# A flamingo block (WKV, FFN, cross attention, MoE) on one core: order of the maxima and the big fill on SP's queue, and the shared expert's first products

## The reference

```python
x = x + tanh(g_xattn[0]) * wkv(layernorm(x), ctx)
x = x + tanh(g_ffn[0]) * ffn(layernorm(x))                  # 704 hidden, silu gate
x = x + tanh(g_xattn[1]) * attention(layernorm(x), ctx)     # 16 heads of 8, source and target mask, softmax
x = x + tanh(g_ffn[1]) * moe(layernorm(x))
# attention: q, k, v are projections of 128 channels over 256 positions (a batch is read as 128 x 256)
dot = einsum('bhdt,bhds->bhts', q, k) / sqrt(8)
dot = mask * dot - (1 - mask) * 1e6
out = einsum('bhts,bhds->bhdt', softmax(dot) * mask, v)
# moe: 8 experts, top 1, 256 slots each, 352 hidden, and a shared expert that takes every token
shared = (silu(xt @ sw1) * (xt @ sw3)) @ sw2
```

## Time and profile before

| what | value |
|---|---|
| median of three runs | 559.36 us |
| the profiled execution | 558.33 us |
| its span | 556.5 us |
| mean granted clock of TensorE | 0.972 |
| the profile's block 2 (attention with the FFN's end) | about 153 to 407.6 us |
| from the experts' block to the end | 407.6 to 556.5 us |

### The profile page before, as it was taken

The page is one execution under the profiler, slowest core; times in us unless marked ns, Lnnn a source line. Parts: engine busy times, 40 slices in busy tenths (PEclk is TensorE's granted clock), DMA queues, the critical chain, the costliest instruction groups (busy, mean ns, idle before and its releaser), DMA issues. The chain is left out here.

```text
span 556.5 us, 10469 instructions
## 1 busy us (share of the span) xinstructions
PE 483.7 (87%) x3384; PEld 264.7 (48%) x3384; DVE 379.6 (68%) x768; ACT 247.5 (44%) x478; POOL 229.2 (41%) x303
## 2 busy tenths in 40 slices
PE   2859999998898788988898989787979989899994
PEld 2634564745533433333333433332434545688873
DVE  4986879788589777788788888795757433333331
ACT  2732233121232177878788888677711100133321
POOL 2753224142367165666555565412110730024424
PEclk9987999999999979999999999899999999999998
DMA  7747600000175525555556665510050241168753
GB/s 214 214 145 166 104 1 0 1 1 2 57 195 143 130 57 150 147 143 143 141 141 147 162 156 135 146 28 5 1 157 1 91 165 47 58 167 185 196 127 38
DMA packets 67254, 59.94 MB, mean 108 GB/s; under 512 B 10048, under 2 KB 62256, under 8 KB 67216
## 3 DMA queue, kind: packets, MB, share of 16 engines
q1 hardware_dynamic: 63424, 55.24, 36.9%
q0 software_dynamic: 3072, 4.21, 4.4%
q10 hardware_dynamic: 720, 0.00, 0.1%
HBM read 38.90 MB, written 22.50 MB: 110 GB/s over the span
## 5 line engine op out<-in xcount | busy, mean ns | idle before, releaser
L1175 DVE TENSOR_REDUCE MX<-psum 128x2 f32<-128x512 f32 x256 | 161.3, 683 | 34.4 <-PE psum L1054 33.4
L1215 ACT ACTIVATE HP<-psum 128x512 f32<-128x512 f32 x256 | 137.5, 598 | 56.4 <-PE psum L1068 55.4
L1054 PE MATMUL psum<-QKA 60*128 60x256 bf16 x512 | 83.7, 281 | 13.8 <-DVE MX L1175 10.1
L1068 PE MATMUL psum<-QKA 60*128 60x256 bf16 x512 | 79.4, 281 | 16.1 <-DMA QKA<-max_scr 12.6
L1141 PE MATMUL psum<-HP,VP 128*32 128x256 f32 x1024 | 84.0, 402 | 0.2 <-ACT HP L1215 0.2
L512 PE MATMUL psum<-space_a,space_w 128*128 128x512 f32 x160 | 75.0, 618 | 1.1 <-ACT space_a L497 0.8
L1054 PEld LDWEIGHTS psum<-QKA 60*128 60x128 bf16 x512 | 35.9, 96 | 69.3 <-DVE MX L1175 47.9
L1736 POOL DMA_INDIRECT out_x<-OE,to_u x16 | 25.0, 1564 | 75.7 <-ACT OE L1777 73.2
L512 PEld LDWEIGHTS psum<-space_a,space_w 128*128 128x128 f32 x160 | 30.3, 197 | 37.9 <-issue 35.3
L525 ACT ACTIVATE space_a<-psum,hgs 128x512 f32<-128x512 f32 (+1 forms) x24 | 15.6, 651 | 70.3 <-PE psum L512 47.8
L1875 PE MATMUL psum<-XT,WE 128*128 128x256 f32 (+1 forms) x192 | 44.3, 380 | 2.4 <-ACT XT L1761 1.6
(11 more groups left out here) (186 smaller groups left out, 735.3 us busy)
## 6 DMA issues: line engine op xcount, KB each, us to landing
QKA<-stack_scr SPq DMA_DIRECT2D x32, 480.0 KB, 5.4
stack_scr<-PARTS SPq DMA_DIRECT2D x32, 192.0 KB, 2.0
WE<-in_W SPq DMA_DIRECT2D x16, 352.0 KB
stack_scr<-PARTS SPq DMA_DIRECT2D x32, 128.0 KB, 1.9
XD<-dispatched SPq DMA_DIRECT2D x8, 258.0 KB, 3.7
X<-in_x SPq DMA_DIRECT2D x4, 512.0 KB, 5.6
CTX<-in_ctx SPq DMA_DIRECT2D x4, 512.0 KB, 8.2
MB<-in_mask SPq DMA_DIRECT2D x16, 128.0 KB, 5.7
```

Source lines behind the costliest of these rows:

```text
L1054: return pe.matmul(to[:, tt * T:(tt + 1) * T], QKA[rows, k, 0, h, tt * P:(tt + 1) * P], QKA[rows, k, 1, h, :], start=True, stop=True)
L1068: return pe.matmul(to[:, (m % 2) * T:(m % 2 + 1) * T], QKA[rows, k, 1, h, st * P:(st + 1) * P], QKA[rows, k, 0, h, :], start=True, stop=True)
L1175: dve.tensor_reduce(MX[:, par, head_of(n), :], src[:, :].rearrange("p (a s) -> p a s", a=2), axis=AX.X, op=ALU.max).then_inc(a_red, 1)
L1215: act.activation(PT[:, i % 2, st, 2 * half:2 * half + 2, :].rearrange("p j t -> p (j t)"), TBK3[THIRDS[m]], ACT.Exp).then_inc(a_exp, 1)
```

## The change

Seven edits.

1. SP, in each batch of the attention: the big fill is issued behind the maxima's store, the mask load and the maxima's way back, instead of ahead of them.
2. The turning of the maxima (mxT) goes from the end of slot 0 to slot 1, ahead of that slot's scores; it waits for the copy QK of batch b+4, since both use bank 7. The query projection goes from slot 6 to slot 7, and its copy QK on ScalarE from slot 7 to slot 0 of the next batch. NM goes from slot 0 to slot 1, behind that slot's exponentials.
3. Ahead of the first batch: the projection and QK of batch 4 and VectorE's Z3 for it are done before the slots; the projection of batch 3 is later.
4. The one wait of TensorE for both halves of the FFN's last x2 becomes a wait per score bank.
5. The layer norm statistics of the last group (dve_stats3) are cut in five steps and stand in slots of batches 0 to 2 (LAST_STATS); pool_power3 for it stands in batch 2.
6. Five of the shared expert's 24 products (group 0: piece 0 both sides, piece 1 both sides, piece 2's gate side) stand in the last slots of the attention (SHARED).
7. In block 3, HS has two buffers, and the products of group 1 are spread over the router's stretches. The loops over the groups on TensorE and VectorE are written out, ScalarE's covers groups 2 and 3.

```diff
--- before.py
+++ after.py
...
@@ -179,6 +181,16 @@
+        def gu_shared(pe, g, i, side, first=False):
+            m = width(i, EH)
+            if not first and side == 0:
+                pe.wait_ge(m_h, NH * (g - 1) + i + 1)
+            for h in range(2):
+                last = pe.matmul(bank[2 * i + side][0:m, :], (wsh1, wsh3)[side][:, h, i * P:i * P + m],
+                                 ZT4[:, h, bass.ds(GT * g, GT)], start=(h == 0), stop=(h == 1))
+            if side == 1:
+                last.then_inc(m_gu, 1)
+
...
@@ -661,13 +674,24 @@
+            def dve_one_of_last(dve, ch, i):
+
+                if i < GB:
+                    ch.do(dve.bn_stats(stats3[:, i, :], X[:, GB * G3 + i, :]))
+                    return
+                ch.wait()
+                alone(dve)
+                for t in range(GB):
+                    ch.do(dve.bn_aggr(mv3[:, GB * G3 + t, :], stats3[:, t, :]))
+                ch.wait()
+                dve.tensor_scalar(veps3[:, GB * G3:B], mv3[:, GB * G3:B, 1], EPS, None, ALU.add).then_inc(a_var, 1)
+
...
-            G3 = NG - 1
@@ -892,9 +916,9 @@
-                            pe.wait_ge(a_qk, 1)
-                            pe_proj_q(pe, 0, 2, QB[0])
...
+                            pe.wait_ge(s_x2, 1 + 2 * G3)
+                            pe_proj_q(pe, 0, 2)
@@ -1117,6 +1141,8 @@
+                        if first(GB * to_turn[0] + to_turn[1]) and p == 0:
+                            pe.wait_ge(s_x2, 1 + 2 * G3 + n + 1)
@@ -1160,7 +1186,7 @@
-                    pool.wait_ge(a_rstd, NG)
+                    pool.wait_ge(a_rstd, b // GB + 1 if isinstance(b, int) else NG)
@@ -1327,6 +1353,8 @@
+                SHARED = {(B - 1, 7): [(0, 0)], (B, 0): [(0, 1)], (B, 1): [(1, 0), (1, 1)], (B, 4): [(2, 0)]}
+                LAST_STATS = [2, 4, 10, 12, 18]
@@ -1346,8 +1374,6 @@
-                            if there(b, 3):
-                                sp_fill(sp, *at(g, k, 3))
@@ -1356,6 +1382,8 @@
+                            if there(b, 3):
+                                sp_fill(sp, *at(g, k, 3))
@@ -1375,7 +1403,7 @@
-                                act_qk(act, 2, QB[0])
+                                act_qk(act, 2)
@@ -1384,6 +1412,7 @@
+                        act_qk(act, AHEAD_Q)
@@ -1392,12 +1421,10 @@
-                            if p == 0 and there(b, 1):
+                            if p == 0 and not first(b) and there(b, AHEAD_Q):
+                                act_qk(act, b + AHEAD_Q)
+                            if p == 1 and there(b, 1):
...
-                            if p == 2 and first(b):
-                                act_qk(act, AHEAD_Q)
-                            if p == 7 and there(b, AHEAD_Z):
-                                act_qk(act, b + AHEAD_Z)
@@ -1426,18 +1453,17 @@
-                        pool_power3(pool, G3)
...
-                            if p == 0 and not first(b) and there(b, AHEAD_Q):
+                            if p == 0 and there(b, AHEAD_Q):
...
-                            if p == 2 and first(b):
-                                pool_masked(pool, *at(g, k, AHEAD_Q))
+                            if p == 3 and isinstance(b, int) and b == 2:
+                                pool_power3(pool, G3)
@@ -1457,25 +1483,26 @@
-                            if (b, p) == (0, 0):
-                                pe.wait_ge(a_qk, AHEAD_V)
...
+                            if (b, p) == (1, 4):
+                                pe.wait_ge(a_nm, 1)
+                                pe_proj_q(pe, 1, 0)
...
-                            if i == 1:
+                            if i == 3:
+                                pe.wait_ge(a_qk, AHEAD_V)
...
-                        pe.wait_ge(s_x2, 1 + 2 * NG)
@@ -1483,6 +1510,12 @@
+                            if p == 1 and there(b, 1):
+                                if there(b, AHEAD_Q):
+                                    pe.wait_ge(a_qk, b + AHEAD_Q + 1)
+                                else:
+                                    pe.wait_ge(a_x3, b - 1)
+                                pe_mxT(pe, *at(g, k, 1))
@@ -1492,21 +1525,6 @@
-                            if p == 0 and there(b, 1):
-                                if there(b, AHEAD_Q):
-                                    pe.wait_ge(a_qk, b + AHEAD_Q + (0 if first(b) else 1))
-                                else:
-                                    pe.wait_ge(a_x3, b - 1)
-                                pe_mxT(pe, *at(g, k, 1))
-                            if p == 1 and first(b):
-                                pe.wait_ge(a_nm, 2)
-                                pe_proj_q(pe, *at(g, k, AHEAD_Q))
-                            if p == 6 and there(b, AHEAD_Z):
-                                if first(b):
-                                    pe.wait_ge(a_qk, AHEAD_Z)
-                                else:
-                                    pe.wait_ge(a_x3, b)
-                                pe_proj_q(pe, *at(g, k, AHEAD_Z))
@@ -1515,6 +1533,17 @@
+                            if p == 7 and there(b, AHEAD_Z):
+                                if first(b):
+                                    pe.wait_ge(a_nm, 2)
+                                else:
+                                    pe.wait_ge(a_x3, b)
+                                pe_proj_q(pe, *at(g, k, AHEAD_Z))
+                            if isinstance(b, int) and (b, p) in SHARED:
+                                if (b, p) == (B - 1, 7):
+                                    pe.wait_ge(m_zt, 2 * G3)
+                                for piece, side in SHARED[(b, p)]:
+                                    gu_shared(pe, 0, piece, side, first=True)
@@ -1543,19 +1572,19 @@
+                        dve_z3(dve, AHEAD_Q)
...
-                        dve_stats3(dve, ln3, G3)
...
-                            if p == 1 and first(b):
-                                dve_z3(dve, AHEAD_Q)
...
+                            if isinstance(b, int) and 8 * b + p in LAST_STATS:
+                                dve_one_of_last(dve, ln3, LAST_STATS.index(8 * b + p))
@@ -1616,7 +1645,7 @@
-            HS = sbp("HS", [P, NH, GT])
+            HS = sbp("HS", [P, 2, NH, GT])
...
@@ -1745,14 +1772,16 @@
-                    tanh_shared(0, 0, first=True)
-                    tanh_shared(0, 1, first=True)
+                    for i in range(NH):
+                        tanh_shared(0, i, first=True)
+                    tanh_shared(1, 0)
...
-                    tanh_shared(0, 2, first=True)
-                    with act.Fori(1, NG) as g:
+                    tanh_shared(1, 1)
+                    tanh_shared(1, 2)
+                    with act.Fori(2, NG) as g:
...
@@ -1812,43 +1831,44 @@
-                                    last = pe.matmul(bank[6 + k][:, b * C:(b + 1) * C], HS[0:m, i, t * P:(t + 1) * P],
+                                    last = pe.matmul(bank[6 + k][:, b * C:(b + 1) * C], HS[0:m, g % 2, i, t * P:(t + 1) * P],
...
+                    gu_shared(pe, 0, 2, 1, first=True)
...
-                        gu_shared(0, 0, side, first=True)
+                        gu_shared(pe, 1, 0, side)
...
-                    for side in range(2):
-                        gu_shared(0, 1, side, first=True)
-
...
-                    gu_shared(0, 2, 0, first=True)
+                    gu_shared(pe, 1, 1, 0)
...
-                    gu_shared(0, 2, 1, first=True)
+                    gu_shared(pe, 1, 1, 1)
+                    gu_shared(pe, 1, 2, 0)
...
-                    with pe.Fori(0, NG - 1) as g:
+                    gu_shared(pe, 1, 2, 1)
+                    pe.wait_ge(m_pos, 1)
+                    down_shared(0)
+                    for g in range(1, NG - 1):
...
-                            gu_shared(g + 1, 0, side)
-                        pe.wait_ge(m_pos, 1)
+                            gu_shared(pe, g + 1, 0, side)
...
-                                gu_shared(g + 1, i, side)
+                                gu_shared(pe, g + 1, i, side)
@@ -1919,15 +1939,16 @@
-                        dve.scalar_tensor_tensor(out=HS[0:m, i, :], in0=H1[0:m, i, :], scalar=0.5,
+                        dve.scalar_tensor_tensor(out=HS[0:m, g % 2, i, :], in0=H1[0:m, i, :], scalar=0.5,
...
+                    hidden_shared(ch, 0, 0)
...
-                    hidden_shared(ch, 0, 0)
...
+                    hidden_shared(ch, 0, 2)
@@ -1965,7 +1986,7 @@
-                    hidden_shared(ch, 0, 2)
+                    hidden_shared(ch, 1, 0)
@@ -2014,14 +2035,15 @@
-                    before = ch.n
-                    with dve.Fori(0, NG - 1) as g:
-                        ch = Chain(dve, m_dve, before + NH * g)
+                    add_shared(0)
+                    for i in range(1, NH):
+                        hidden_shared(ch, 1, i)
+                    for g in range(1, NG - 1):
...
-                    before += NH * (NG - 1)
+                    before = ch.n
```

(14 more changed lines are left out.)

## The result

The changed kernel takes 595.17 us (median of 4 runs, 592.98 to 596.65), the kernel before in the same comparison 559.09 us: a ratio of 1.066 with a 95% interval of 1.059 to 1.074. It is 36 us slower. I had forecast 606 us, range 586 to 620, slower. The profiled execution of the changed kernel spans 594.0 us, 37.5 more than the one before.

What follows compares the result with a forecast made beforehand. TensorE was taken as the bound, held in the attention by DMA waits for the row maxima. On 558.33 us, +51.3 (period), -0.7 (start), +0.5 (last batches) and -3.3 (shared expert) gave 606.1 us, range 586 to 620.

Steps and rivals of the forecast that it cites:

- the sum: Attention batch, from t: NM 3.9, store 6.4, way back 9.2, fill issued 10.1, done 16.9; with the clock 17.4 us.
- Period: Time per attention batch: 17.4 us instead of 13.45, paid at the starts of batches 1 to 13, +51.3 us.
- t to the store: From a batch's first transposed score to issue of the maxima's store: 6.4 us, plus 0.5 for the lower clock.
- store to way back: On SP's queue, from issuing the maxima's store to issuing their way back, mask load between: 2.8 us, down from 6.3.
- way back to fill: On SP's queue, from issuing the maxima's way back to issuing the big fill: 0.9 us.
- fill: From issue of batch b+3's stacked operands (960 KB) to landing: 6.85 us, at most about 1 us more.
- The wait: TensorE at a batch's first score waits 4 us and more for the fill, some 13 times.
- The other signs for the period: In the profile after: fill issued 10 to 11 us behind t, store landing under 3 us, periods 17 to 18 us.
- Wait at the start: Attention's first score waits for only the first of two x2 steps, no longer both: -0.7 us.
- Shared expert and the last batches: Five products moved into attention's last slots: 6.0 us later there, 8.6 saved behind, 0.7 gained; last batches +0.5 for clock.
- The clock: Rival: TensorE stays at the lower clock for most of a batch; period 18.5 to 19.5, 620 to 633 us, chance 0.05.
- The hidden fill: Rival: the fill lands before the next batch needs it; period 12.0 to 12.4, time 541 us, chance 0.05.

Runs made afterwards that it cites:

- the two experiments built on the kernel before: Kernel before with only SP's order changed: fill issued behind the maxima's way back, 564.26 us; fill right behind the maxima's store, 543.91 us.
- all six experiments built on it: Changed kernel with fill first 552.05 us; early maxima 558.33; both 551.19; fill right behind store 568.94; that with early maxima 538.48; that without products in attention 540.69.
- the run without them: Changed kernel with early maxima and order store, fill, way back (538.48 us), its five shared-expert products moved back to the experts' block: 540.69 us.
- the last kernels: Fill right behind the maxima's store, ahead of the way back: changed kernel with early maxima 538.48 us, kernel before 543.91 us.

## Why the prediction was right, and what was mis-sized

The mechanism is the one in the sum: the fill behind the maxima's landing, the maxima late, and a fill too long for what is left. The runs undid each half and got the time back.

*Period, 17.4 forecast, 16.83 measured from batch 1 on* (16.6 with batch 0). Piece by piece:

| piece | forecast | batch 1 | mean of batches 1 to 12 |
|---|---|---|---|
| t to the store | 6.9 (6.4 and 0.5 for the clock) | 7.27 | 7.39 |
| store to way back | 2.8 | 1.54 | 1.61 |
| way back to fill | 0.9 | 0.77 | 0.94 |
| fill | 6.85 | 6.78 | 6.89 |

The clock's part of the first piece is about 1.0, the upper end of what I had given, not 0.5. The second piece is the term that failed. I had read it from one batch, the one that seemed like the new place, with a mask load and nothing big ahead. In the changed kernel eleven of twelve batches have 1.5 to 1.6, most with the same mask load between. The kernel before had the number too, in batch 13, behind the last fill and without a mask load:

```profile
370.36 0.32 SPq L1282 DMA_DIRECT2D max_scr<-NP  x1
371.89 0.55 SPq L1289 DMA_DIRECT2D QKA<-max_scr  x2
```

In batch 0 the store took 2.7 us to land there, and 3.1 and 3.2 in the two experiments built on the kernel before, but 1.4 to 1.5 in the changed kernel and in all six experiments built on it; what holds it is not known. Over twelve periods the measured sum is 6.8 us less than forecast.

*The wait.* I had written that TensorE idles over 4 us each time. It waits 2.7 in the mean, because part of the longer period is spent working at 1.2 GHz, not waiting: TensorE is busy 20 us more. The sum did not use the 4 us. The other signs for the period came close: the fill leaves at t+9.9 in the mean (10 to 11 forecast), the periods are 16.8 (17 to 18), the store lands in 1.5 (under 3).

*Batch 0* took 14.2 us, not 17.4: its slot has no QK (done ahead of the slots) and no AV, the clock was at the full level up to 203, and the store left at t+5.0. I had taken all 13 batches as alike; 3.2 us. The two misses, 6.8 and 3.2, are 10.0 of the 10.3 us by which the profiled execution grew less than forecast (37.5 against 47.8). Within the period luck helped: the way back taken 1.2 us too late was in part made up by the first piece taken 0.5 too short.

*Wait at the start* -0.2 against -0.7: the wait for VectorE is gone, but the first score's row shows 0.88 us of "issue", idle time without a releaser.

*Shared expert and the last batches.* +7.4 and -10.0 against +6.5 and -9.3; the run without them confirms the net (2.2 against 2.6) and both terms (6.5 against 6.0, 9.4 against 8.6). No stall of an unknown queue as at 443.39 stands in the changed kernel's chain; why it went is not known.

*By the rule* of the Trainium skill ("DMA: Bandwidth & Descriptors", "Anatomy of one DMA"; a fit for the GpSimd path), the estimate for the fill is 4.3 us, and the period would have been 14.8. The traces disagree: in the seven kernels where a batch of the attention waited for the fill, TensorE started on it 6.4 to 8.2 us behind its issue, 6.9 in the mean in the changed one.

*The rivals.* The clock does not stay low: it is back at the full level 3 to 6 us into a batch. The hidden fill was refuted as computed, and the last kernels show what it would have brought: 12.2 to 12.4 a batch.

## What to carry to other kernels

On an in-order DMA queue, do not put a transfer that needs most of a period behind a wait for the landing of another; put it behind the other's issue. Before an order on a queue is changed, write down for each transfer the first moment at which its data are there and the last at which they may land: here the fill, issued at t+3.5, was done at t+10.4, 1.4 us before the next batch's first straight score (299.58 in the kernel before, t+11.8), and behind the maxima's round trip it left at t+9.6, 6 us later. Two edits that cost 1 and 7 us each can cost 44 us together when both eat from the same slack.

## What the runs showed of the hardware

A DMA of 24 KB lands in 1.5 us with no fill ahead of it in nearly all batches (2.2 to 3.4 in a few), in about 6 us when it is issued right behind the 960 KB fill, and in 4.7 us when it is issued 2.6 us behind the fill. That it waits for the bytes ahead of it is an inference from these three numbers.

The time from the fill's issue to the score that waited for it is 6.5 to 7.3 us in the changed kernel, 6.9 in the mean, with the 24 KB just ahead of it and 768 KB of stores issued 2 to 3 us behind it; the kernel before, where the stores come later, has 6.85. Where the 128 KB mask load and the maxima's way back follow right behind it, it is 6.8 to 7.9, 7.1 in the mean (the run with late maxima and the order store, fill, way back).

In all 13 batches of the changed kernel TensorE waited 1.9 to 3.2 us for the fill, and the granted clock was 0.50 until 3 to 6 us into the batch. The path to the next fill lies in that stretch and took about 1 us longer than at the full clock (7.17 against 6.20 us), so the low clock made the period, and with it the next wait, longer.
